# Moving transposed-tile and V copies from ScalarE to VectorE, and the feed-forward work inside an attention block

## The chip, the cores and the metric

The kernel runs on 8 NeuronCores of one Trainium2 chip. Every core runs the same program on its own 4 sequences of the batch of 32. The time is device microseconds (us) of the slowest core, for one execution.

## What is computed

For x of shape (32, 2048, 1024), with four 1024 x 1024 attention matrices and a feed-forward layer of 3072 hidden columns whose int32 weights are scaled by 1/127:

```python
xn = _layernorm(x, axis=-1)
# s: attention of xn
q = _l2norm(proj(Wq)); k = _l2norm(proj(Wk)); v = proj(Wv)   # 16 heads of 64
attn = jnp.einsum('bhqd,bhkd->bhqk', q, k)
mask = (rel < 0) | (rel >= WINDOW)      # rel = key - query, WINDOW = 128
attn = softmax(attn + alibi, masked)
s = (attn @ v) @ Wo
# g: silu of the feed-forward layer of xn
g = _silu((_silu(xn @ wg.T) * (xn @ wu.T)) @ wd.T)
x = x + s * g
```

A query attends to itself and the 127 keys behind it in the sequence's order, so a block of 128 queries needs two blocks of 128 keys: its own and the next.

## The kernel before

**Tiles.** A core's 4 sequences of 2048 tokens are cut into tiles of 512 tokens, 4 per sequence, 16 in all (`n_iters`). Before the first tile a prologue transposes all weights to bf16 with TensorE and stores them in HBM scratch (`prep_attn`, `prep_gu`, `prep_wd`), normalizes the first two tiles' x and computes K and V of tile 0.

**One tile** (`tile(g, wq_s)`) does the following, in this order: Q of tile g (`proj_eh`, L484, then `norm_apply`, L439 to L452, then `kq_transpose`, L465 and L472); the layer-norm sums of tile g+2 (`ln_stats`, L369 to L395, only where g+2 is still a tile, so 14 times in the loop); K of tile g+1 the same way as Q; V of tile g+1 (`proj_eh`, L484, and a copy out of PSUM, L724); four attention blocks of 128 queries (`attn_qb`); the layer norm's application for tile g+2 (`ln_apply`, L401 and L406) and its transposition (`xn_T`, L420 and L427); the 12 down-projection groups (`down_group`, L550); and the epilogue (`epilogue_tc`, L565 to L573), whose ScalarE and VectorE work runs beside the next tile's Q projection.

**The filler.** `filler(n)` puts n feed-forward units (`ffn_unit`) into the program at the place where it is called. A unit is 8 gate matmuls into PSUM tensor psB (L507), a Silu on ScalarE (L515) that reads them, 8 up matmuls (L524), and a multiplication on VectorE (L532) that writes HID. Each tile has 24 units. Two units alternate between two banks each of psB; all else of a tile uses psA.

**One attention block** (`attn_qb(g, qb, wo_s, filler)`). `ci` is 0 for the queries' own block of keys and 1 for the next one. The last block of a sequence has no second block of keys; that is 4 of the 64 blocks. For each ci, 16 score matmuls (L596) write all four banks of psA, four exponentials on ScalarE (L606) read one bank each and write PT, and four multiplications on VectorE (L611) put the position factors EB on PT. Then 32 matmuls with V (L627) write psA again, VectorE takes the reciprocal of the sums (L640) and normalizes into TM (L645), TensorE transposes TM (8 matmuls, L657), ScalarE copies that to AOF (L664), 16 matmuls with Wo follow (L673), and ScalarE copies their two banks to SBS (L681). Three filler calls stand in a block: behind the exponentials of each ci, and behind L645.

**What sets the order.** There is no scheduler. `_Plan.op` appends every operation to its engine's list in the order in which the Python code is run, and each engine works through its list strictly in that order. A wait is a `wait_ge` on a semaphore ahead of the instruction. It comes from the buffers that an operation reads and writes: `bpsA[b]` and `bpsB[b]` stand for the PSUM banks, `bPT`, `bTM4`, `bXN`, `bKF`, `bQF`, `bVP`, `bHID12` for the SBUF tensors. So the place of a filler call in the code sets its place in the lists of TensorE, ScalarE, VectorE and of the DMA queue at once. The tables of ScalarE's functions (L606, L515, L446 and L389 are listed with ACT_TABLE_LOAD) are put in by the compiler in front of an ACTIVATE whose function is not in the table set that is loaded.

Of the kernel before, what the change touches and what calls it, by code (L numbers as in the profile page):

```python
# [20 lines left out]
DCN = D // 128  # L21
# [107 lines left out]
def build_nc(n_iters=NTILES, dbg=False):  # L129
# [29 lines left out]
    P = _Plan()  # L159
# [6 lines left out]
    with stack:  # L166
# [246 lines left out]
        def xn_T(gt, tcs):  # L413
            p1 = gt % 2
            for tc in tcs:
                def tfn(e, tc=tc):
                    last = None
                    bc = psA[:, 512 * tc:512 * tc + 512].bitcast(BF16)
                    for dc in range(DCN):
                        last = e.transpose(  # L420
                            bc[:, 128 * dc:128 * dc + 128],
                            TM[:, 1024 * tc + 128 * dc:1024 * tc + 128 * dc + 128],
                            IDT[:, :])
                    return last
                P.op("pe", tfn, reads=[bTM4[tc], bIDT], writes=[bpsA[tc]],
                     tag=f"xnT{gt}_{tc}")
                P.op("act", (lambda e, tc=tc, p1=p1: e.copy(  # L427
                    XN[p1][:, :].rearrange("p (dc t) -> p dc t", dc=DCN)[:, :, 128 * tc:128 * tc + 128],
                    psA[:, 512 * tc:512 * tc + 512].bitcast(BF16).rearrange(
                        "p (dc t) -> p dc t", dc=DCN))),  # L430
                    reads=[bpsA[tc]], writes=[bXN[p1][tc]], tag=f"xnEv{gt}_{tc}")

        def norm_apply(g1, which, eh, tc):
# [25 lines left out]
        def kq_transpose(g1, DST, bDST, tag, tcs):  # L459
            for tc in tcs:  # L460
                def tfn(e, tc=tc):
                    last = None
                    bc = psA[:, 512 * tc:512 * tc + 512].bitcast(BF16)
                    for ec in range(DCN):
                        last = e.transpose(  # L465
                            bc[:, 128 * ec:128 * ec + 128],
                            TM[:, 1024 * tc + 128 * ec:1024 * tc + 128 * ec + 128],
                            IDT[:, :])
                    return last
                P.op("pe", tfn, reads=[bTM4[tc], bIDT], writes=[bpsA[tc]],  # L470
                     tag=f"{tag}{g1}_{tc}")
                P.op("act", (lambda e, tc=tc, DST=DST: e.copy(  # L472
                    DST[:, :].rearrange("p (ec t) -> p ec t", ec=DCN)[:, :, 128 * tc:128 * tc + 128],
                    psA[:, 512 * tc:512 * tc + 512].bitcast(BF16).rearrange(
                        "p (ec t) -> p ec t", ec=DCN))),
                    reads=[bpsA[tc]], writes=[bDST], tag=f"{tag}Ev{g1}_{tc}")

        def proj_eh(g1, eh, wslot, p1, tag):
# [104 lines left out]
        def attn_qb(g, qb, wo_s, filler):  # L583
            p, pn = g % 2, (g + 1) % 2
            j = g % TILES_PER_SEQ
            have_c1 = (qb < 3) or (j < 3 and g + 1 < n_iters)
            for ci in range(2 if have_c1 else 1):
                kc = qb + ci
                kpar, kcc = (p, kc) if kc < TCN else (pn, 0)
                for par in range(2):  # L590
                    def skfn(e, par=par, kpar=kpar, kcc=kcc, qb=qb):
                        last = None
                        r0 = 64 * par
                        for h in range(par, 16, 2):
                            ecb = 512 * (h // 2)
                            last = e.matmul(  # L596
                                psA[:, 128 * h:128 * h + 128],
                                KF[kpar][r0:r0 + 64, ecb + 128 * kcc:ecb + 128 * kcc + 128],
                                QF[r0:r0 + 64, ecb + 128 * qb:ecb + 128 * qb + 128],
                                start=True, stop=True)  # L600
                        return last
                    P.op("pe", skfn, reads=[bKF[kpar], bQF],
                         writes=[bpsA[0], bpsA[1], bpsA[2], bpsA[3]],
                         tag=f"qk{g}_{qb}_{ci}_{par}")
                for b in range(4):
                    P.op("act", (lambda e, b=b, ci=ci: e.activation(  # L606
                        PT[:, 2048 * ci + 512 * b:2048 * ci + 512 * b + 512],
                        psA[:, 512 * b:512 * b + 512], AF.Exp)),
                        reads=[bpsA[b]], writes=[bPT[ci][b]],
                        tag=f"exp{g}_{qb}_{ci}_{b}")  # L610
                    P.op("dve", (lambda e, b=b, ci=ci: e.tensor_tensor(  # L611
                        PT[:, 2048 * ci + 512 * b:2048 * ci + 512 * b + 512],
                        PT[:, 2048 * ci + 512 * b:2048 * ci + 512 * b + 512],
                        EB[:, 2048 * ci + 512 * b:2048 * ci + 512 * b + 512],
                        ALU.mult)),
                        reads=[bEB, bPT[ci][b]], writes=[bPT[ci][b]],
                        tag=f"emul{g}_{qb}_{ci}_{b}")
                filler(1)

            for b in range(4):  # L620
                def avfn(e, b=b, qb=qb, have_c1=have_c1, p=p, g=g):
                    last = None
# [25 lines left out]
                st(RZ0, 16).unsqueeze(2).broadcast_to([128, 16, 64]), ALU.mult)),  # L648
                reads=[bpsA[0], bpsA[1], bpsA[2], bpsA[3], bRZ],
                writes=[bTM4[qb]], tag=f"aonrm{g}_{qb}")  # L650
            filler(1)

            def aotfn(e, qb=qb):
                last = None
# [32 lines left out]
        def tile(g, wq_s):  # L687
            p, pn = g % 2, (g + 1) % 2
# [6 lines left out]
            def filler(n):  # L695
                for _ in range(n):
                    if fstate[0] < HCN:
                        ffn_unit(g, fstate[0], pf)
                        fstate[0] += 1
# [13 lines left out]
            if g + 1 < n_iters:  # L713
# [7 lines left out]
                wv_s = load_wa("wv", 0, f"wv0_{g}"), load_wa("wv", 1, f"wv1_{g}")  # L721
                for eh in range(2):
                    for tc in proj_eh(g + 1, eh, wv_s[eh], pn, "vproj"):
                        P.op("act", (lambda e, eh=eh, tc=tc, pn=pn: e.copy(  # L724
                            VP[pn][:, :].rearrange("p (kc h c) -> p kc h c", kc=4, c=65)[:, tc, 8 * eh:8 * eh + 8, 0:64],
                            psA[:, 512 * tc:512 * tc + 512].rearrange(
                                "p (h c) -> p h c", h=8))),
                            reads=[bpsA[tc]], writes=[bVP[pn]],
                            tag=f"vEv{g}_{eh}_{tc}")
                    filler(1)  # L730
# [36 lines left out]
            if has_ln:  # L767
                xn_T(g + 2, range(TCN))
# [50 lines left out]
        wv_s = load_wa("wv", 0, "wv0_p"), load_wa("wv", 1, "wv1_p")  # L819
        for eh in range(2):  # L820
            for tc in proj_eh(0, eh, wv_s[eh], 0, "vproj"):
                P.op("act", (lambda e, eh=eh, tc=tc: e.copy(
                    VP[0][:, :].rearrange("p (kc h c) -> p kc h c", kc=4, c=65)[:, tc, 8 * eh:8 * eh + 8, 0:64],
                    psA[:, 512 * tc:512 * tc + 512].rearrange(
                        "p (h c) -> p h c", h=8))),
                    reads=[bpsA[tc]], writes=[bVP[0]], tag=f"vEvp_{eh}_{tc}")
        prep_attn("wq")
        prep_attn("wo")
# [77 lines left out]
```

How the kernel before makes its waits and increments, by code:

```python
        def load_wa(nm, eh, tag):  # L226
            s = wa_i[0] % 3
            wa_i[0] += 1
            ap, bf = WA[s], bWA[s]
            src_ap = wT[nm][eh]
            P.op("sp", (lambda e, sem, ap=ap, src_ap=src_ap:
                        e.dma_start(ap[:, :], src_ap).then_inc(sem, 16)),
                 reads=[bWT[nm]], writes=[bf], tag=tag)
            return ap, bf
# [4 lines left out]
        def load_gu_hc(nm, hc, tag):  # L239
            s = gu9_i[0] % 9
            gu9_i[0] += 1
            ap, off = WGU[s // 3], 1024 * (s % 3)
            bf = bGU9[s]
            P.op("sp", (lambda e, sem, ap=ap, off=off, src=wT[nm][hc]:
                        e.dma_start(ap[:, off:off + 1024], src).then_inc(sem, 16)),
                 reads=[bWT[nm]], writes=[bf, bWGU[s // 3]], tag=tag)
            return (ap, off), bf
# [591 lines left out]
        def run(eng_obj, name):  # L839
            for (waits, fn, evt, tag, nd) in P.ops[name]:
                for w in waits:
                    eng_obj.wait_ge(sems[w.sem], w.val)
                if nd > 0:
                    fn(eng_obj, sems[evt.sem])
                else:
                    inst = fn(eng_obj)
                    if evt.used:
                        inst.then_inc(sems[evt.sem], 1)
            if name == "gp":
                for i in range(NDMASEM):
                    s_ = f"gp{i}"
                    if counts.get(s_, 0):
                        eng_obj.wait_ge(sems[s_], counts[s_])
```

## Time and profile before

| what | value |
|---|---|
| time before, median of 2 runs | 4488.03 us (4459.62 to 4516.44) |
| the profiled execution | 4467.43 us |
| its span on the slowest core | 4465.9 us (cores 4438.0 to 4465.9) |
| mean granted TensorE clock, cores 0 to 7 | 0.924 to 0.928 |
| busy: TensorE matmul, ScalarE, VectorE | 78%, 45%, 27% |

The profile is one execution seen by the hardware profiler. PE is TensorE's matmuls, PEld its weight loads, ACT is ScalarE, DVE is VectorE, POOL is GpSimd. L484 is line 484 of the kernel. A matmul's duration is its latency: matmuls overlap, so 8 matmuls of 128x512 that are listed with 380 ns each take 1.9 us together. The span begins with the prologue (about 600 us) and then has 16 tiles of about 249 us each.

### The profile page before, as it was taken

To read this page: it belongs to the slowest core of one execution; us is meant where nothing else is said; L and a number is where in the kernel's file an instruction comes from. 1 tells how busy PE (TensorE), PEld (TensorE's weight loads), DVE (VectorE), ACT (ScalarE), POOL (GpSimd) and SP (SyncE) were. 2 spreads that over 40 slices of the span, in tenths; PEclk is the share of its full clock that TensorE was granted. 3 is DMA by queue.
4 is the path that set the end of the run, shared out by engine and by line. 5 is a ranking of instruction groups with operands and counts; after the bars stand their busy time and mean duration, and the time that the engine had idled before them with its cause. 6 is when DMAs were issued, how large, how long until landed. Compare 5 with 4: busy or idle time off the path is not lost.

```text
span 4465.9 us, 59790 instructions; the slowest of 8 cores (4438.0 to 4465.9 us)
## 1 busy us (share of the span) xinstructions
PE 3499.2 (78%) x20160; PEld 1670.1 (37%) x20160; DVE 1219.4 (27%) x2230; ACT 1989.2 (45%) x2803; POOL 127.6 (3%) x276
## 2 busy tenths in 40 slices
PE   1422298888879888888888888888879888888887
PEld 1221144343434344343434343443434343444443
DVE  0100032323323232323333232323232232324141
ACT  4322163544635263544535363635545353635352
POOL 1111000000000000000000000000000000000000
PEclk9755599999999999999999999999999999999999
DMA  6576543434343433434343534434343534334342
GB/s 151 113 132 112 140 142 116 160 110 153 116 158 112 165 125 126 152 111 164 111 144 111 184 114 139 147 114 161 111 155 106 172 114 151 137 102 171 99 150 91
DMA packets 276419, 596.38 MB, mean 134 GB/s; under 512 B 71072, under 2 KB 71072, under 8 KB 258720
## 3 DMA queue, kind: packets, MB, share of 16 engines
q1 hardware_dynamic: 236192, 464.63, 32.4%
q0 software_dynamic: 39936, 127.94, 10.9%
q8 instruction: 175, 2.87, 0.3%
q14 instruction: 116, 0.95, 0.1%
HBM read 558.92 MB, written 60.82 MB: 139 GB/s over the span
## 4 chain that ended last, share of the span: by engine, by line
PE 56%; DMA 13%; ACT 12%; issue 9%; DVE 8%; POOL 0%; DVEq 0%; ACTq 0%; SPq 0%; POOLq 0%
PE psB L507 12%; PE psB L524 11%; PE psA L484 8%; PE psA L550 7%; PE psB L550 6%; PE psA L673 5%; DMA WD<-wdT_s 4%; PE psA L596 3%; DVE STAT L442 3%; DMA wgT_s<-WGU 2%; DMA wuT_s<-WGU 2%; PE psA L627 2%; DVE GBUF L569 2%; ACT GBUF L373 2%; ACT GBUF L369 2%
## 5 line engine op out<-in xcount | busy, mean ns | idle before, releaser
L484 PE MATMUL psA<-WA,XN 128*128 128x512 bf16 x3072 | 744.8, 403 | 243.9 <-DVE TM L452 177.5
L524 PE MATMUL psB<-XN,WGU 128*128 128x512 bf16 x3072 | 732.3, 382 | 31.9 <-ACT GBUF L565 29.7
L507 PE MATMUL psB<-XN,WGU 128*128 128x512 bf16 x3072 | 727.1, 380 | 3.8 <-ACT GBUF L565 3.8
L484 PEld LDWEIGHTS psA<-WA,XN 128*128 128x128 bf16 x3072 | 309.4, 102 | 673.3 <-issue 366.2
L550 PE MATMUL psA<-WD,HID 128*128 128x512 bf16 x1536 | 404.0, 386 | 96.3 <-ACT XN L427 38.7
L532 DVE TENSOR_TENSOR HID<-psB,TSC 128x512 bf16<-128x512 f32 x384 | 262.5, 691 | 726.5 <-PE psB L524 340.5
L524 PEld LDWEIGHTS psB<-XN,WGU 128*128 128x128 bf16 x3072 | 300.3, 98 | 401.7 <-issue 45.8
L507 PEld LDWEIGHTS psB<-XN,WGU 128*128 128x128 bf16 x3072 | 283.5, 98 | 331.2 <-issue 10.7
L550 PE MATMUL psB<-WD,HID 128*128 128x512 bf16 x1536 | 403.5, 386 | 0.0
L565 ACT ACTIVATE GBUF<-psA,CST 128x1024 f32<-128x1024 f32 x32 | 35.6, 1113 | 822.9 <-PE psB L550 777.2
L611 DVE TENSOR_TENSOR PT<-PT,EB 128x512 bf16<-128x512 bf16 x496 | 210.6, 425 | 565.4 <-ACT PT L606 541.9
L442 DVE TENSOR_REDUCE STAT<-SQ 128x8 f32<-128x512 f32 x256 | 173.3, 677 | 590.4 <-ACT SQ L439 590.1
L569 DVE TENSOR_TENSOR GBUF<-GBUF,SBS 128x1024 f32<-128x1024 f32 x64 | 78.4, 1226 | 902.6 <-ACT GBUF L565 902.6
L515 ACT ACTIVATE TSC<-psB,CST 128x512 bf16<-128x512 f32 x384 | 258.8, 686 | 141.8 <-PE psB L507 78.9
L673 PE MATMUL psA<-WA,AOF 128*128 128x512 bf16 x1024 | 231.3, 379 | 88.8 <-ACT AOF L664 88.8
L550 PEld LDWEIGHTS psA<-WD,HID 128*128 128x128 bf16 x1536 | 138.6, 98 | 324.3 <-issue 192.8
L606 ACT ACTIVATE PT<-psA 128x512 bf16<-128x512 f32 x496 | 256.0, 603 | 1.4
L278 PE MATMUL psA<-IDT,WD 128*128 128x128 bf16 x640 | 79.8, 304 | 225.0 <-DMA WD<-wg 50.6
L515 ACT ACT_TABLE_LOAD x186 | 238.6, 1283 | 3.6
L550 PEld LDWEIGHTS psB<-WD,HID 128*128 128x128 bf16 x1536 | 152.6, 99 | 189.0 <-issue 13.4
L606 ACT ACT_TABLE_LOAD x124 | 159.1, 1283 | 113.3 <-PE psA L596 112.2
L596 PE MATMUL psA<-QF,KF 64*128 64x128 bf16 x1984 | 149.9, 215 | 62.5 <-ACT SBS L681 42.4
(67 smaller groups left out, 2484.9 us busy)
## 6 DMA issues: line engine op xcount, KB each, us to landing
WGU<-wgT_s SPq DMA_DIRECT2D x384, 256.0 KB, 2.8
WGU<-wuT_s SPq DMA_DIRECT2D x384, 256.0 KB, 2.8
WD<-wdT_s SPq DMA_DIRECT2D x192, 512.0 KB, 3.6
XL<-x POOLq DMA_DIRECT2D x16, 2048.0 KB, 10.3
WA<-wkT_s SPq DMA_DIRECT2D x32, 1024.0 KB, 8.8
WA<-wvT_s SPq DMA_DIRECT2D x32, 1024.0 KB, 8.0
XE<-x POOLq DMA_DIRECT2D x16, 2048.0 KB, 9.8
WA<-wqT_s SPq DMA_DIRECT2D x32, 1024.0 KB, 6.0
```

What stands on the lines that cost most here:

```text
L442: P.op("dve", (lambda e, SS8=SS8, sqo=sqo: e.tensor_reduce(st(SS8, 8).rearrange("p (h u) -> p h u", u=1), SQ[:, sqo:sqo + 512].rearrange(" ...
L484: last = e.matmul(psA[:, 512 * tc:512 * tc + 512], XN[p1][:, 512 * dc + 128 * tc:512 * dc + 128 * tc + 128], wap[:, 512 * dc:512 * dc + 51 ...
L507: last = e.matmul(psB[:, go:go + 512], gap[:, goff + 128 * dc:goff + 128 * dc + 128], XN[p][:, 512 * dc:512 * dc + 512], start=(dc == 0), ...
L515: P.op("act", (lambda e, hc=hc, go=go: e.activation(TSC[:, 512 * (hc % 2):512 * (hc % 2) + 512], psB[:, go:go + 512], AF.Silu, scale=CST[: ...
L524: last = e.matmul(psB[:, uo:uo + 512], uap[:, uoff + 128 * dc:uoff + 128 * dc + 128], XN[p][:, 512 * dc:512 * dc + 512], start=(dc == 0), ...
L532: P.op("dve", (lambda e, hc=hc, uo=uo: e.tensor_tensor(HID[:, 512 * hc:512 * hc + 512], psB[:, uo:uo + 512], TSC[:, 512 * (hc % 2):512 * ( ...
L550: last = e.matmul(pt[:, off + 512 * dh:off + 512 * dh + 512], HID[:, 512 * hc + 128 * tc:512 * hc + 128 * tc + 128], wdap[:, 1024 * i + 51 ...
L569: P.op("dve", (lambda e, tc=tc: e.tensor_tensor(GBUF[:, :], GBUF[:, :], SBUF_S[:, 1024 * tc:1024 * tc + 1024], ALU.mult)), reads=[bG, bSB4 ...
L596: last = e.matmul(psA[:, 128 * h:128 * h + 128], KF[kpar][r0:r0 + 64, ecb + 128 * kcc:ecb + 128 * kcc + 128], QF[r0:r0 + 64, ecb + 128 * q ...
L606: P.op("act", (lambda e, b=b, ci=ci: e.activation(PT[:, 2048 * ci + 512 * b:2048 * ci + 512 * b + 512], psA[:, 512 * b:512 * b + 512], AF. ...
L611: P.op("dve", (lambda e, b=b, ci=ci: e.tensor_tensor(PT[:, 2048 * ci + 512 * b:2048 * ci + 512 * b + 512], PT[:, 2048 * ci + 512 * b:2048 ...
L673: last = e.matmul(psA[:, 1024 + 512 * half:1024 + 512 * half + 512], AOF[:, 128 * ec:128 * ec + 128], wap[:, 512 * ec:512 * ec + 512], sta ...
```

## The change

Two things are changed.

First, four copies out of PSUM go from ScalarE's list to VectorE's, at the same place in the program: the transposed layer norm output (L427), transposed Q and K (L472), V in the tile loop (L724) and V in the prologue (L822). `e.copy` on ScalarE becomes `e.tensor_scalar_mul` by 1.0 on VectorE.

Second, the three filler calls of an attention block move. The one behind the exponentials and EB multiplications of a ci now stands between the score matmuls and the exponentials of that ci, and the third, which stood behind the normalization L645, now stands ahead of the matmuls with V. Lines 606 to 645 of before are one higher in the changed kernel.

```diff
-                P.op("act", (lambda e, tc=tc, p1=p1: e.copy(
+                P.op("dve", (lambda e, tc=tc, p1=p1: e.tensor_scalar_mul(
                     XN[p1][:, :].rearrange("p (dc t) -> p dc t", dc=DCN)[:, :, 128 * tc:128 * tc + 128],
                     psA[:, 512 * tc:512 * tc + 512].bitcast(BF16).rearrange(
-                        "p (dc t) -> p dc t", dc=DCN))),
+                        "p (dc t) -> p dc t", dc=DCN), 1.0)),
                     reads=[bpsA[tc]], writes=[bXN[p1][tc]], tag=f"xnEv{gt}_{tc}")
...
@@ attn_qb
                         tag=f"qk{g}_{qb}_{ci}_{par}")
+                filler(1)
                 for b in range(4):
                     P.op("act", (lambda e, b=b, ci=ci: e.activation(
...
                         tag=f"emul{g}_{qb}_{ci}_{b}")
-                filler(1)
-
+
+            filler(1)
             for b in range(4):
                 def avfn(e, b=b, qb=qb, have_c1=have_c1, p=p, g=g):
...
                 writes=[bTM4[qb]], tag=f"aonrm{g}_{qb}")
-            filler(1)
 
             def aotfn(e, qb=qb):
```

L472, L724 and L822 are edited as L427 is.

**ScalarE's list, one attention block.** Before, from the exponentials of ci 0 to the copies into SBS (PT holds the exponentials, TSC is the Silu's output, AOF and SBS are the block's last copies):

```order
L606 ACTIVATE PT<-psA 128x512 x4
L515 ACTIVATE TSC<-psB,CST 128x512
L606 ACTIVATE PT<-psA 128x512 x4
L515 ACTIVATE TSC<-psB,CST 128x512 x2
L664 COPY AOF<-psA 128x1024
L681 CAST SBS<-psA 128x512 x2
```

The same block in the changed kernel:

```order
L515 ACTIVATE TSC<-psB,CST 128x512
L607 ACTIVATE PT<-psA 128x512 x4
L515 ACTIVATE TSC<-psB,CST 128x512
L607 ACTIVATE PT<-psA 128x512 x4
L515 ACTIVATE TSC<-psB,CST 128x512
L664 COPY AOF<-psA 128x1024
L681 CAST SBS<-psA 128x512 x2
```

Each Silu has moved from behind the four exponentials of its ci to ahead of them; the third is still behind the last exponentials.

**VectorE's list, one attention block.** Before, from the EB multiplications of ci 0 (PT<-PT,EB) to the third unit's multiplication into HID:

```order
L611 TENSOR_TENSOR PT<-PT,EB 128x512 x4
L532 TENSOR_TENSOR HID<-psB,TSC 128x512
L611 TENSOR_TENSOR PT<-PT,EB 128x512 x4
L532 TENSOR_TENSOR HID<-psB,TSC 128x512
L640 RECIPROCAL STAT<-psA 128x16
L645 TENSOR_TENSOR TM<-psA,STAT 128x1024
L532 TENSOR_TENSOR HID<-psB,TSC 128x512
```

The same block in the changed kernel:

```order
L532 TENSOR_TENSOR HID<-psB,TSC 128x512
L612 TENSOR_TENSOR PT<-PT,EB 128x512 x4
L532 TENSOR_TENSOR HID<-psB,TSC 128x512
L612 TENSOR_TENSOR PT<-PT,EB 128x512 x4
L532 TENSOR_TENSOR HID<-psB,TSC 128x512
L641 RECIPROCAL STAT<-psA 128x16
L646 TENSOR_TENSOR TM<-psA,STAT 128x1024
```

Each unit's multiplication stands ahead of the EB multiplications of its ci, and the third unit's has moved ahead of the reciprocal and the normalization.

**TensorE's list, from the matmuls with V to the next block's scores.** Before (L627 the matmuls with V, L657 the transposes, L673 the matmuls with Wo):

```order
L627 MATMUL psA<-VP,PT 128x65 x32
L507 MATMUL psB<-XN,WGU 128x512 x8
L524 MATMUL psB<-XN,WGU 128x512 x8
L657 MATMUL psA<-IDT,TM 128x128 x8
L673 MATMUL psA<-WA,AOF 128x512 x16
```

In the changed kernel, from the third unit on:

```order
L507 MATMUL psB<-XN,WGU 128x512 x8
L524 MATMUL psB<-XN,WGU 128x512 x8
L628 MATMUL psA<-VP,PT 128x65 x32
L657 MATMUL psA<-IDT,TM 128x128 x8
L673 MATMUL psA<-WA,AOF 128x512 x16
```

The unit that stood between the matmuls with V and the transposes of their normalized result now stands ahead of both. The score matmuls and the first two units keep their places in TensorE's list.

## Rows read from the trace of the kernel before

**Rows 1.** What TensorE waited for: us in total, times, longest us.

```profile
PE psA L484 <- DVE TM L452: 177.5, 33, 9.2
...
PE psA L550 <- ACT XN L427: 38.7, 14, 2.8
```

**Rows 2.** Timeline, one attention block: start, length, engine, instruction, [idle before <- releaser].

```profile
2420.77 0.60 PE L596 MATMUL psA<-QF,KF 64*128 64x128 bf16 x8 [0.88 <-ACT SBS L681]
...
2422.05 1.90 PE L507 MATMUL psB<-XN,WGU 128*128 128x512 bf16 x8
2422.20 1.28 ACT L606 ACT_TABLE_LOAD   x1 [1.58 <-PE psA L596]
2423.50 2.06 ACT L606 ACTIVATE PT<-psA 128x512 bf16<-128x512 f32 x4
...
2425.71 0.60 PE L596 MATMUL psA<-QF,KF 64*128 64x128 bf16 x8
...
2426.88 0.69 ACT L515 ACTIVATE TSC<-psB,CST 128x512 bf16<-128x512 f32 x1
...
2427.67 0.69 DVE L532 TENSOR_TENSOR HID<-psB,TSC 128x512 bf16<-128x512 f32 x1 [1.57 <-ACT TSC L515]
...
2428.88 2.06 ACT L606 ACTIVATE PT<-psA 128x512 bf16<-128x512 f32 x4
...
2429.57 1.90 DVE L611 TENSOR_TENSOR PT<-PT,EB 128x512 bf16<-128x512 bf16 x4 [1.22 <-ACT PT L606]
...
2430.46 1.66 PE L627 MATMUL psA<-VP,PT 128*128 128x65 bf16 x32
...
2431.96 1.89 PE L507 MATMUL psB<-XN,WGU 128*128 128x512 bf16 x8
...
2433.72 0.25 DVE L640 RECIPROCAL STAT<-psA 128x16 f32<-128x16 f32 x1
2434.06 0.69 ACT L515 ACTIVATE TSC<-psB,CST 128x512 bf16<-128x512 f32 x1 [1.12 <-DVE STAT L640]
2434.07 1.23 DVE L645 TENSOR_TENSOR TM<-psA,STAT 128x1024 bf16<-128x1024 f32 x1
...
2435.55 0.61 PE L657 MATMUL psA<-IDT,TM 128*128 128x128 bf16 x8
...
2437.51 3.61 PE L673 MATMUL psA<-WA,AOF 128*128 128x512 bf16 x16 [1.35 <-ACT AOF L664]
...
2442.00 1.36 PE L596 MATMUL psA<-QF,KF 64*128 64x128 bf16 x16 [0.88 <-ACT SBS L681]
```

**Rows 3.** Timeline of the same tile and the next: waits around the normalizations.

```profile
2472.45 1.02 PE L550 MATMUL psA<-WD,HID 128*128 128x512 bf16 x4 [2.76 <-ACT XN L427]
...
2538.72 6.59 PE L484 MATMUL psA<-WA,XN 128*128 128x512 bf16 x22 [4.33 <-DVE TM L452]
...
2558.63 4.31 ACT L472 COPY QF<-psA 128x1024 bf16<-128x1024 bf16 x4
...
2563.41 1.06 ACT L369 ACTIVATE GBUF<-XL 128x1024 f32<-128x1024 f32 x1
...
2581.13 10.01 PE L484 MATMUL psA<-WA,XN 128*128 128x512 bf16 x32 [8.82 <-DVE TM L452]
```

**Rows 4.** Groups by line and shape: busy us, mean ns of one, idle before.

```profile
L611 DVE TENSOR_TENSOR PT<-PT,EB 128x512 bf16<-128x512 bf16 x496 | 210.6, 425 | 565.4 <-ACT PT L606 541.9
...
L645 DVE TENSOR_TENSOR TM<-psA,STAT 128x1024 bf16<-128x1024 f32 x64 | 78.4, 1225 | 6.7
...
L472 ACT COPY QF<-psA 128x1024 bf16<-128x1024 bf16 x64 | 64.8, 1012 | 4.3
```

**Rows 5.** Stretches: length, busy us (instructions) of each engine, clock, DMA share, GB/s.

```profile
2535.00:2540.00 5.00, 1.27 (x5) 0.61 (x6) 2.35 (x7) 2.71 (x5) 1.21 (x2) 0.93 0.63 227
2540.00:2545.00 5.00, 5.00 (x19) 1.88 (x17) 3.62 (x10) 1.56 (x5) 0.08 (x1) 0.73 0.55 170
...
2470.00:2475.00 5.00, 2.55 (x12) 1.20 (x13) 0.00 (x0) 2.20 (x3) 0.00 (x0) 1.00 0.86 349
```

More of the change, by code:

```diff
@@ L471, in kq_transpose @@
                      tag=f"{tag}{g1}_{tc}")
-                P.op("act", (lambda e, tc=tc, DST=DST: e.copy(
+                P.op("dve", (lambda e, tc=tc, DST=DST: e.tensor_scalar_mul(
                     DST[:, :].rearrange("p (ec t) -> p ec t", ec=DCN)[:, :, 128 * tc:128 * tc + 128],
                     psA[:, 512 * tc:512 * tc + 512].bitcast(BF16).rearrange(
-                        "p (ec t) -> p ec t", ec=DCN))),
+                        "p (ec t) -> p ec t", ec=DCN), 1.0)),
                     reads=[bpsA[tc]], writes=[bDST], tag=f"{tag}Ev{g1}_{tc}")
@@ L723, in tile @@
                     for tc in proj_eh(g + 1, eh, wv_s[eh], pn, "vproj"):
-                        P.op("act", (lambda e, eh=eh, tc=tc, pn=pn: e.copy(
+                        P.op("dve", (lambda e, eh=eh, tc=tc, pn=pn: e.tensor_scalar_mul(
                             VP[pn][:, :].rearrange("p (kc h c) -> p kc h c", kc=4, c=65)[:, tc, 8 * eh:8 * eh + 8, 0:64],
                             psA[:, 512 * tc:512 * tc + 512].rearrange(
-                                "p (h c) -> p h c", h=8))),
+                                "p (h c) -> p h c", h=8), 1.0)),
                             reads=[bpsA[tc]], writes=[bVP[pn]],
@@ L821, in build_nc @@
             for tc in proj_eh(0, eh, wv_s[eh], 0, "vproj"):
-                P.op("act", (lambda e, eh=eh, tc=tc: e.copy(
+                P.op("dve", (lambda e, eh=eh, tc=tc: e.tensor_scalar_mul(
                     VP[0][:, :].rearrange("p (kc h c) -> p kc h c", kc=4, c=65)[:, tc, 8 * eh:8 * eh + 8, 0:64],
                     psA[:, 512 * tc:512 * tc + 512].rearrange(
-                        "p (h c) -> p h c", h=8))),
+                        "p (h c) -> p h c", h=8), 1.0)),
                     reads=[bpsA[tc]], writes=[bVP[0]], tag=f"vEvp_{eh}_{tc}")
```

## The prediction

> **What bounds the kernel now.** I read the table of waits for TensorE first, then the timeline of one attention block, then the places where the moved copies stand. TensorE is busy for 78% of the span and ScalarE for 45%, so the tile loop is TensorE work with holes in it, and the question is which holes the change closes and which it opens. The reader should see two things in the waits [rows 1]. The largest one, 177.5 us, is the projections (L484) waiting for the normalization L452, a chain of ScalarE and VectorE steps. The down projections wait 38.7 us, 14 times, for ScalarE's copy of XN (L427), one of the copies that are moved.
>
> The timeline of one block [rows 2] shows an order that fits well. Take the first score matmul at 2420.77 as zero; the next block's is at 2442.00, so a block takes 21.23. The gate starts at 1.28, ScalarE does its table load and the four exponentials meanwhile, and the second scores start at 4.94 (2425.71), 0.15 after the last exponential has ended (2423.50 + 2.06 = 2425.56). The unit of 3.46 us (2427.00 to 2430.46) covers the exponentials, and the third unit covers reciprocal and normalization: the transposes follow at 2435.55, 3.59 after that unit's gate. TensorE's only holes in the block are 1.35 ahead of L673 and 0.88 ahead of the next scores.
>
> **The attention block after the change.** TensorE keeps scores, unit, scores, unit in the same order, but the second scores need all four banks of psA, so they need the first four exponentials, and on ScalarE these now stand behind a Silu that needs the gate. I follow the chain with the durations of rows 2. Gate at 1.28; its Silu starts 2.10 after a gate does (2431.96 to 2434.06), so 3.38. The Silu table is loaded already, since the unit before was the last to need one. Silu 0.69, table load 1.30 (2422.20 to 2423.50), exponentials 2.06, release 0.15: the second scores start at 7.58 in place of 4.94. That is a first step of 2.64 lost.
>
> From there: gate 1.29 later at 8.87; ScalarE can go on 2.10 later, at 10.97, and now needs a table load ahead of the Silu (12.27), the Silu (12.96), a load (14.26), the exponentials (16.32), a load again, and the third Silu at 17.62, whose gate has long ended. Its multiplication into HID starts 0.79 after the Silu does (2426.88 to 2427.67), 18.41. VectorE works in order, and behind this multiplication now stand the reciprocal (19.10), the normalization 0.35 later (19.45) and so the transposes 1.48 later (2434.07 to 2435.55), at 20.93. The matmuls with V have been done by then: their last operand is ready at 14.26 + 0.69 + 1.90 = 16.85, and they end near 17.4. From transposes to the next block's scores nothing changes, 6.45 (2435.55 to 2442.00). The block ends at 27.38 in place of 21.23: 6.15 more.
>
> The number of table loads stays four per block. What changes is that all four lie on the path, and that the third unit covers the exponentials while nothing covers the normalization. 60 blocks have two halves: 60 x 6.15 = 369. The 4 blocks at a sequence's end have one, and I take the first step for them, 4 x 2.6 = 10. The lower bound for a block is 5.2, if the waits turn out some 0.2 shorter at each of five hand-overs; the upper one is 6.5.
>
> **The copies.** No row shows VectorE reading bf16 from PSUM. Bounds: 1.23 us as L645 (1024 elements from fp32 PSUM), and twice the 512 elements of L611 at 0.425, so 0.85 or, as part of 0.425 is fixed, somewhat less; ScalarE takes 1.012 [rows 4]. L611 is the nearest row by type, and I take 0.7 to 0.85.
>
> At XN (14 times, where ln_stats runs) the copies end the wait of 2.76 [rows 3]. At 0.75 each the four end about 0.8 earlier, at 1.23 about 1.2 later: -11 us, bounds -11 and +17. The last unit's multiplication is ahead of them on VectorE; that is counted.
>
> At Q, ScalarE spends 4.31 on four copies, then takes a unit's Silu, then starts ln_stats at 2563.41. Once the copies are gone, the Silu can run as soon as its gate ends: that gate follows the transposes at about 2558.3, so 2560.4 by the 2.10 above, and ln_stats starts at about 2561.1, 2.3 earlier. The chain behind it ends in the wait of 8.82 at 2581.13 [rows 3], so this wait becomes 6.5: 14 x 2.3 = -32 us. Bounds: 0, if TensorE then waits for something else in that place, and -60, if the whole 4.31 counts. VectorE has no other work there until the squares come.
>
> K's copies and V's are hidden before and after: each is followed by a unit of 3.46 us or stands beside 7 us of projections, and a bank's copy needs 0.85 to 1.23. I cost them at 0, and the prologue's too. If the cover went, a tile would lose at most the 0.2 by which each copy could be slower.
>
> **TensorE's clock.** The hole between the end of the matmuls with V and the transposes will be 3.5 us, followed by only 0.6 of work and 1.35 of waiting. Rows show a wait of 2.76 without any fall (the stretch 2470 to 2475, clock 1.00), and a wait of 4.33 that ends at 2538.72 with the granted clock falling to its lower level (1.2 GHz) around there: 0.93 and 0.73 in two stretches of 5 us, which is 0.7 + 2.7 = 3.4 us at half [rows 3, 5]. Mine lies between. If the fall comes in each of the 60 blocks, with TensorE at work throughout, the 3.4 us cost 1.7 each, 102 us; if it never comes, 0. Part of such a stretch falls into the wait ahead of L673, so I take 1.0 each, +60. By the Trainium skill, "TensorE: Matmul & The Clock Gate", section "HAM oscillation — how this bites in real kernels", it is gaps that bring the engine down again and again and each burst then starts cold, which speaks for this term; the trace agrees at the 4.33 us wait.
>
> **Sum.** Against the profiled execution, 4467.4: + 369 + 10 - 11 - 32 + 60 = 4863, I say 4860. That execution lies 0.5% under the median of the two runs shown (4488), inside their spread.
>
> **The rivals.**
> A. Only the first step counts: VectorE's late third multiplication is hidden, because the third unit on TensorE runs late enough to cover it. 60 x 2.64 + 10 = 168, - 43: 4592. Against it: the unit ends at 15.8, and the reciprocal waits till 19.1.
>
> B. Not slower: ScalarE is what limits each tile, and every wait that its copies end or push goes. Place: the waits of rows 1, 177.5 + 38.7 = 216. With A's 158 for the blocks: 4467 + 158 - 216 = 4409. It decides where a block loses less than 216 / 60 = 3.6. For it: ScalarE's copies stand ahead of both waits. Against it: the wait of 8.82 holds ln_stats itself, of which no part is moved, and that of 4.33 comes behind no moved copy.
>
> C. The clock stays at the lower level through the attention blocks. Then the two gates that are on the chain take 1.7 more each, the scores 0.6 twice and L673 3.2: 8 per block, 4863 - 60 + 480 = 5280. Against it: the other holes are 2.64 and shorter, like the 2.76 without a fall.
>
> D. A table load costs more than its row. The Trainium skill, "ScalarE: Activation LUTs", section "What ACT_TABLE_LOAD costs", has a drain of about 1.38 us behind each load of 1.28. In this kernel that would put 4 x 1.38 on each block's chain, x 60 = 331: 5190 as an estimate from that page. The trace disagrees: the exponentials start 1.30 after the load does [rows 2]. As a mechanism of rows alone, a second cost as long as the load itself, 4 x 1.28 x 60 = 307, gives 5170.
>
> That the change doesn't do what it says can be excluded: the order of the lists shows it.
>
> **Chances.** Forecast 0.83, A 0.06, B 0.04, C 0.04, D 0.03. For the forecast's own range, low: blocks at 5.2 (-57), no fall of the clock (-60), 4746; high: blocks at 6.5 (+21), the clock in full (+42), copies at 1.23 (+28), 4954. Range 4745 to 4950, which leaves out A to D. Faster by over 2% (about what a measurement of this kernel can tell from no change) 0.01, a part of B; within 2% 0.03, the rest of B; slower 0.96.
>
> **What would show it.** In the profile after: the second scores wait 2.6 for the exponentials (L607), about 160 us in all, a wait that the kernel of before does not have. The transposes L657 wait about 3.5 for L646, some 200 us in all. The third Silu starts 17.6 after the block's first score, a block takes 27.4, and the projections' wait for L452 falls from 177.5 to about 145. The copies on VectorE show 0.7 to 0.85 us. The clock's mean falls below 0.92 if the clock term is right. I am wrong if a block takes under 25 us, if the Silu's table load runs ahead of its wait for the gate (that would take 1.3 off each block), or if the clock in the attention stretches stays at 1.00 (then 4800).

## The result, and the profile after

The changed kernel takes 5039 us (median of 12 executions; 5034.6 to 5042.7 in the undisturbed eight of them) against 4545 for the kernel before in the same comparison (lowest 4451.6). The ratio is 1.1306, 95% interval [1.1291, 1.1322]: 13% slower. The prediction had the sign and the place right, with 4860 us, but its size too small: the time lies above the range's end of 4950. (In some executions of every kernel here, before and after alike, part of the cores show a lower granted clock for long stretches; ratios leave those executions out, and "undisturbed cores" are those of an execution that do not show it.)

The page of the changed kernel, its head, its clock by slices and the busy times:

```profile
span 5038.6 us, 59650 instructions; the slowest of 8 cores (5015.2 to 5038.6 us)
...
PE 3764.0 (75%) x20160; PEld 1759.6 (35%) x20160; DVE 1429.6 (28%) x2550; ACT 1733.5 (34%) x2483; POOL 127.6 (3%) x276
...
PEclk9655889898998989898998989899898989899988
```

ScalarE is 256 us less busy than before, VectorE 210 more, as moved. TensorE has the same 20160 matmuls and is busy 265 us longer. That is the clue: the same matmuls take longer, and the mean granted clock of TensorE is 0.873 on this core, where before has 0.927. The traces of these two profiles show only two levels of the clock, full (2.4 GHz) and half (1.2 GHz), so the time at half can be worked out: (1 - 0.873) x 2 x 5038.6 = 1280 us, before (1 - 0.927) x 2 x 4465.9 = 652.

What TensorE waited for in the changed kernel (us in total, times, longest), which answers to [rows 1]:

```profile
PE psA L657 <- DVE TM L646: 210.9, 64, 3.7
PE psA L596 <- ACT PT L607: 159.6, 60, 2.9
PE psA L484 <- DVE TM L452: 151.9, 34, 6.8
...
PE psA L550 <- DVE XN L427: 26.3, 14, 2.2
```

The first two did not exist before, but for 0.3 us. They are 210.9 / 64 = 3.3 and 159.6 / 60 = 2.7 each, where 3.5 and 2.64 were predicted. The two others have shrunk by 25.6 and 12.4.

One attention block of the changed kernel, from one block's first scores to the next's, which answers to [rows 2]:

```profile
2621.21 1.37 PE L596 MATMUL psA<-QF,KF 64*128 64x128 bf16 x16
...
2622.51 1.90 PE L507 MATMUL psB<-XN,WGU 128*128 128x512 bf16 x8
...
2624.62 0.69 ACT L515 ACTIVATE TSC<-psB,CST 128x512 bf16<-128x512 f32 x1 [4.17 <-PE psB L507]
2625.33 1.28 ACT L607 ACT_TABLE_LOAD   x1
...
2628.83 2.17 PE L596 MATMUL psA<-QF,KF 64*128 64x128 bf16 x16 [2.69 <-ACT PT L607]
...
2630.93 3.59 PE L507 MATMUL psB<-XN,WGU 128*128 128x512 bf16 x8
...
2634.72 1.28 ACT L515 ACT_TABLE_LOAD   x1 [6.03 <-PE psB L507]
...
2641.39 0.69 ACT L515 ACTIVATE TSC<-psB,CST 128x512 bf16<-128x512 f32 x1
2642.18 0.69 DVE L532 TENSOR_TENSOR HID<-psB,TSC 128x512 bf16<-128x512 f32 x1 [1.57 <-ACT TSC L515]
2642.79 0.25 DVE L641 RECIPROCAL STAT<-psA 128x16 f32<-128x16 f32 x1
...
2644.62 0.61 PE L657 MATMUL psA<-IDT,TM 128*128 128x128 bf16 x8 [3.35 <-DVE TM L646]
...
2646.69 6.44 PE L673 MATMUL psA<-WA,AOF 128*128 128x512 bf16 x16 [1.46 <-DMA WGU<-wgT_s]
...
2654.01 1.36 PE L596 MATMUL psA<-QF,KF 64*128 64x128 bf16 x16 [0.88 <-ACT SBS L681]
```

Read against the steps: the second scores start at 7.62 (2628.83 - 2621.21), predicted 7.58. Until then the chain is exact. Then the same 16 score matmuls take 2.17 in place of 1.37, and the 8 gate matmuls 3.59 in place of 1.90. From here each thing is late by what the slow matmuls add: the second Silu's table load comes at 13.5 (predicted 10.97), the transposes at 23.4 (20.93). And behind the second wait the 16 matmuls with Wo take 6.44 in place of 3.61. (The 1.46 ahead of them is the usual wait for AOF, 0.1 longer for a transfer that came last.) The block is 32.8 long; the prediction said 27.4 by the steps and added 1.0 for the clock. It is one of the longer blocks: over the 48 blocks of this trace that have two halves and another block right behind them, the mean from first scores to first scores is 31.6.

The stretches of this block (length, busy us of PE, PEld, DVE, ACT and POOL, clock, DMA share, GB/s) show the granted clock:

```profile
2621.21:2631.00 9.79, 6.80 (x50) 4.00 (x50) 3.08 (x6) 4.04 (x6) 0.00 (x0) 0.87 0.44 146
2631.00:2645.00 14.00, 10.65 (x72) 5.10 (x72) 4.48 (x8) 7.29 (x9) 0.00 (x0) 0.84 0.37 114
2645.00:2654.00 9.00, 6.67 (x21) 2.23 (x18) 0.00 (x0) 2.19 (x3) 0.00 (x0) 0.62 0.10 29
```

Half-speed time is twice the missing share: 2.5, 4.5 and 6.8 us, together 13.8 of 32.8.

The copies on VectorE (busy us, mean ns, idle before):

```profile
L724 DVE TENSOR_SCALAR VP<-psA 128x512 bf16<-128x512 f32 x120 | 83.3, 694 | 119.8 <-PE psA L484 119.8
...
L472 DVE TENSOR_SCALAR QF<-psA 128x1024 bf16<-128x1024 bf16 x64 | 44.1, 689 | 5.4 <-DVE QF L472 0.5
```

0.689 us for 1024 bf16 elements from PSUM, just under the low end of what was taken (0.7 to 0.85), where ScalarE took 1.012. V's copies from fp32 take 0.694 on VectorE, ScalarE needed 0.587, and nothing waits for them.

### The profile page after: what moved, and what is told of

It reads as the page before. It is cut to its first block, busy times and chain, and to the rows that moved or that the text cites. A ratio compares the mean times of both kernels' runs of the same rounds, so it can differ in the third digit from the quotient of the medians.

```text
span 5038.6 us, 59650 instructions; the slowest of 8 cores (5015.2 to 5038.6 us)
## 1 busy us (share of the span) xinstructions
PE 3764.0 (75%) x20160; PEld 1759.6 (35%) x20160; DVE 1429.6 (28%) x2550; ACT 1733.5 (34%) x2483; POOL 127.6 (3%) x276
## 4 chain that ended last, share of the span: by engine, by line
PE 43%; ACT 22%; DMA 12%; DVE 11%; issue 10%; DVEq 0%; ACTq 0%; POOL 0%; SPq 0%; POOLq 0%
PE psB L507 10%; PE psA L673 7%; PE psA L484 6%; PE psA L550 5%; PE psB L550 5%; ACT PT L607 4%; DMA WD<-wdT_s 4%; ACT L515 4%; PE psA L596 3%; PE psB L524 3%; ACT L607 3%; DVE STAT L442 3%; ACT TSC L515 3%; DMA wgT_s<-WGU 2%; DMA wuT_s<-WGU 2%
## 5 line engine op out<-in xcount | busy, mean ns | idle before, releaser
L507 PE MATMUL psB<-XN,WGU 128*128 128x512 bf16 x3072 | 821.8, 416 | 4.1 <-ACT GBUF L565 4.1
L524 PE MATMUL psB<-XN,WGU 128*128 128x512 bf16 x3072 | 756.1, 391 | 29.7 <-ACT GBUF L565 29.7
L524 PEld LDWEIGHTS psB<-XN,WGU 128*128 128x128 bf16 x3072 | 310.0, 101 | 432.0 <-issue 101.4
L507 PEld LDWEIGHTS psB<-XN,WGU 128*128 128x128 bf16 x3072 | 306.8, 104 | 407.2 <-issue 118.6
L673 PE MATMUL psA<-WA,AOF 128*128 128x512 bf16 x1024 | 361.3, 530 | 88.7 <-ACT AOF L664 85.8
L596 PE MATMUL psA<-QF,KF 64*128 64x128 bf16 x1984 | 178.2, 240 | 220.2 <-ACT PT L607 159.6
L596 PEld LDWEIGHTS psA<-QF,KF 64*128 64x128 bf16 x1984 | 134.0, 104 | 298.2 <-issue 298.2
L673 PEld LDWEIGHTS psA<-WA,AOF 128*128 128x128 bf16 x1024 | 126.2, 128 | 305.8 <-issue 274.3
```

The lines of the kernel that those rows point to most:

```text
L507: last = e.matmul(psB[:, go:go + 512], gap[:, goff + 128 * dc:goff + 128 * dc + 128], XN[p][:, 512 * dc:512 * dc + 512], start=(dc == 0), ...
L524: last = e.matmul(psB[:, uo:uo + 512], uap[:, uoff + 128 * dc:uoff + 128 * dc + 128], XN[p][:, 512 * dc:512 * dc + 512], start=(dc == 0), ...
L596: last = e.matmul(psA[:, 128 * h:128 * h + 128], KF[kpar][r0:r0 + 64, ecb + 128 * kcc:ecb + 128 * kcc + 128], QF[r0:r0 + 64, ecb + 128 * q ...
L673: last = e.matmul(psA[:, 1024 + 512 * half:1024 + 512 * half + 512], AOF[:, 128 * ec:128 * ec + 128], wap[:, 512 * ec:512 * ec + 512], sta ...
```

## The experiments

The theory after the result: the chain is as predicted, and what was too small is the clock. Each of a block's two waits brings it down, and the matmuls that follow are on the chain. The rival: the chain through ScalarE and VectorE itself is longer, and the low clock only goes with idling. A second question was what each part of the change costs alone.

**The two parts alone.** `copies_only` undoes the filler calls:

```diff
-                filler(1)
                 for b in range(4):
                     P.op("act", (lambda e, b=b, ci=ci: e.activation(
...
                         tag=f"emul{g}_{qb}_{ci}_{b}")
-
-            filler(1)
+                filler(1)
             for b in range(4):
...
                 writes=[bTM4[qb]], tag=f"aonrm{g}_{qb}")
+            filler(1)
```

> The four copies on VectorE, the filler calls where they were. Theory (the moved filler calls are the whole loss, and the copies a small gain): the projections' wait for L452 goes from 177.5 to about 150 and the wait for XN from 38.7 to about 26, so 4415 us, ratio about 0.99. Rival (VectorE's copies are part of the loss, by delaying the HID multiplications): above 4480.

Measured: ratio 0.9881, interval [0.978, 0.9982], lowest execution 4402 us against 4453 for the kernel before in the same comparison. On core 2 of its profile (4411 us) the waits are 151.1 for L452 and 25.8 for XN, as expected. The theory holds, and the copies are a gain of about 50 us, though by the interval it could be almost nothing or 2%.

`fillers_only` is the kernel of before with the three filler calls moved as in the change.

> The copies stay on ScalarE, the three filler calls moved. Theory: the copies' gain of about 40 us is missing, 5080 us. Rival (copies and fillers act on each other, ScalarE being the longer for its copies only now): 5150 or more.

Measured: 5207 us, with two cores at 5204 and 5206 and the six others at 5078 to 5110. The four cores without any disturbed stretch are at 5078 to 5093, and on these the theory's 5080 is met. It is one profile of two executions, so it is weaker than the others. But the two parts add up within some 10 us: 5035 + 50 = 5085.

**Which filler call.** `third_back` takes the changed kernel and puts only the third call back behind the normalization:

```diff
-            filler(1)
             for b in range(4):
                 def avfn(e, b=b, qb=qb, have_c1=have_c1, p=p, g=g):
...
                 writes=[bTM4[qb]], tag=f"aonrm{g}_{qb}")
+            filler(1)
```

> The changed kernel with the third filler call back behind L646; the two others stay ahead of the exponentials. Theory (the late exponentials make the loss, and the third unit only decides where the hole stands): the matmuls with V start at about 16.9 after the block's first scores where the changed kernel has its transposes at 23.4, the hole of 3 us moves ahead of them, the block stays above 30 us, 4950 to 5040 us. Rival (the third call's place costs the 3.3 us of the wait ahead of L657 by itself): 211 us less, 4830.

Measured: 4951 and 4970 us, ratio 1.1091 [1.0991, 1.119]. What TensorE waited for in it:

```profile
PE psA L627 <- DVE PT L612: 172.1, 66, 3.4
PE psA L596 <- ACT PT L607: 157.7, 60, 2.7
```

The wait of 210.9 ahead of the transposes is gone, and 172.1 stand ahead of the matmuls with V instead: the hole moved by one step. So with the exponentials late, the third call's place decides where the second hole is, and not whether there is one.

`pair_back` is the reverse: the ci calls back, the third call ahead of the matmuls with V.

```diff
-                filler(1)
                 for b in range(4):
                     P.op("act", (lambda e, b=b, ci=ci: e.activation(
...
                         tag=f"emul{g}_{qb}_{ci}_{b}")
+                filler(1)
```

> The changed kernel with the two calls of the ci loop back behind the EB multiplications; the third call stays ahead of the matmuls with V. By the rows of before the third unit's up ends at 13.1, the matmuls with V at 14.7, reciprocal and normalization at 16.4 and the transposes start at 16.7 in place of 14.8: a block of 23.1. Theory: 4415 + 64 x 1.9 = 4535 us, and no fall of the clock in the blocks (hole of 2.0). Rival (the third call costs its 3.3 us whatever the others do, and a fall of the clock with it): 4700.

Measured: 4668 us, undisturbed cores 6 and 7 at 4585 and 4586; two executions only, so no ratio. Two waits of its profile:

```profile
PE psA L484 <- DVE TM L452: 149.5, 34, 7.0
PE psA L657 <- DVE TM L646: 125.9, 64, 2.3
```

125.9 / 64 = 2.0 per block, as worked out (1.9). But core 6 has a clock of 0.908, so (1 - 0.908) x 2 x 4584.8 = 844 us at half, some 200 more than before. My claim that a hole of 2.0 makes no fall was wrong, and the time is 50 us above the 4535 on the best cores. The rival's 4700 is missed too, but its fall of the clock is there. On core 6 the clock is at half in 60 of the 64 blocks, somewhere between the matmuls with V and the end of those with Wo. One of them, with the wait of 1.94 ahead of L657 and, 0.6 of matmuls later, one of 1.68 ahead of L673:

```profile
2428.96 0.61 PE L657 MATMUL psA<-IDT,TM 128*128 128x128 bf16 x8 [1.94 <-DVE TM L646]
2431.24 5.08 PE L673 MATMUL psA<-WA,AOF 128*128 128x512 bf16 x15 [1.68 <-ACT AOF L664]
```

The same block on core 0 has the same two waits and keeps its clock (15 matmuls of L673 in 3.40 us, granted clock 1.00):

```profile
2430.78 0.61 PE L657 MATMUL psA<-IDT,TM 128*128 128x128 bf16 x8 [1.95 <-DVE TM L646]
...
2433.07 3.40 PE L673 MATMUL psA<-WA,AOF 128*128 128x512 bf16 x15 [1.68 <-ACT AOF L664]
```

The parts of the move overlap. Against the 4402 of `copies_only`, the third call alone costs about 180 us (4585), the other two alone about 550 (`third_back`, 4951), and all three together 633.

**The clock by itself.** Four kernels leave the changed kernel's order as it is and give TensorE idle matmuls in the waits, whose result nobody reads. They write the psB bank that the next gate writes, which is free by then. The code is shortened here:

```diff
+        def idle_mm(n):
+            bank = fs_ref[0][0] % 2
+            def dmf(e, n=n, bank=bank):
+                for _ in range(n):
+                    last = e.matmul(psB[:, 512 * bank:512 * bank + 512],
+                                    IDT[:, :], EB[:, 0:512], start=True, stop=True)
+                return last
+            P.op("pe", dmf, reads=[bIDT, bEB], writes=[bpsB[bank]], tag="idle")
...
                 filler(1)
+                if ci == 0 and have_c1:
+                    idle_mm(11)
                 for b in range(4):
...
                 writes=[bTM4[qb]], tag=f"aonrm{g}_{qb}")
+            idle_mm(15)
```

> The changed kernel with idle matmuls (128x512, into the psB bank that the next gate writes, their result is not used) on TensorE in the two waits of a block with two halves: 11 (2.4 us) ahead of the second scores and 15 (3.2 us) between the matmuls with V and the transposes, the latter in all 64. They make nothing wait that does not wait already. Theory (the two waits bring TensorE's clock to its lower level, and the work of the chain that then runs at half speed is the part of the loss that the prediction had too small): clock back to 1.00 in the blocks, a block of 27.4 to 27.6, 4790 to 4810 us. Rival (the chain through ScalarE and VectorE is longer than predicted, and the lower clock only goes with idling): 5030 us or more, since work was added.

Measured: 4792 to 4806 us, ratio 1.0713 [1.0609, 1.0818]. Some 1600 matmuls were added and 240 us have gone. The theory's number is met within its range, and the rival is out: over the 48 blocks of core 0 that have two halves and another block right behind them, a block takes 27.35 us on average, and the steps of the prediction gave 27.38. Core 0's clock, and the second wait of a block in its timeline, where L589 is the idle matmuls:

```profile
core 0: 4789.3 us, clock 0.939
```

```profile
2601.12 3.40 PE L589 MATMUL psB<-EB,IDT 128*128 128x512 bf16 x15
...
2604.38 0.61 PE L674 MATMUL psA<-IDT,TM 128*128 128x128 bf16 x8
...
2606.34 3.61 PE L690 MATMUL psA<-WA,AOF 128*128 128x512 bf16 x16 [1.35 <-ACT AOF L681]
```

The matmuls with Wo take 3.61 again. At half: (1 - 0.939) x 2 x 4789.3 = 584 us on core 0, up to 614 on the three other undisturbed cores, where the cores of the changed kernel have 1244 to 1289. So 630 to 705 us at half speed cost 243 us of time, 0.34 to 0.39 of each. All of it on the chain would cost 0.5 of each, since work that fills a us at half speed takes half a us at full; so some 70 to 80% of it was on the chain, and the rest fell on waits or beside it.

`hole1` fills only the wait ahead of the second scores.

> Only the 11 idle matmuls ahead of the second scores. Theory: the fall behind this wait goes (scores, gate and up of the second half at full speed, at most 2.3 us of a block), that behind the transposes' wait stays: about 4920 us. Rival (the clock follows the mean load of the block): no change in one half, the same small rise in both, 5000 us or more.

Measured: 4951 us (lowest; the profiled execution 4994, its six undisturbed cores at 4925 to 4933), ratio 1.111 [1.0976, 1.1245]. `hole2` fills only the wait ahead of the transposes.

> Only the 15 idle matmuls ahead of the transposes. Theory: L673 back from 6.4 us to 3.6, up to 3 us of a block, the fall behind the exponentials' wait stays: about 4900 us. Rival as for the kernel with the first wait filled: 5000 us or more.

Measured: 4863 and 4873, ratio 1.0877 [1.077, 1.0984]. Against the 5035 of the changed kernel the first gives back 84 us (about 100 on undisturbed cores) and the second 172, where both filled give 243. So the two falls are nearly independent, and both were wanted to get the whole. I had expected 115 and 135: the second costs more than the first, because it hits L673, which stands wholly on the chain. Its 16 matmuls take 5.8 us on average in `hole1` and 3.6 in `hole2` (core 0 of each).

The traces show which blocks have time at half speed. Out of 64 blocks (60 of which have the first wait), on the core with the fewest and the one with the most:

| kernel | from the first scores to the matmuls with V | from there to the end of Wo |
|---|---|---|
| before | 0 to 1 | 0 |
| changed | 56 to 59 | 64 |
| `hole1` | 0 | 64 |
| `hole2` | 31 to 50 | 0 to 1 |
| both filled (`both_holes`) | 0 to 1 | 0 to 2 |
| half of each (`half_holes`, next) | 9 to 13 | 10 to 16 |

Each fall goes with its own wait, and the rival of the mean load is out. Filling the second wait also saves some blocks the first fall.

`half_holes` fills half of each wait (6 and 8 idle matmuls).

> The changed kernel with idle matmuls for half of each wait of a block: 6 (1.3 us) ahead of the second scores and 8 (1.7 us) ahead of the transposes, so 1.3 and 1.6 us of waiting stay. Theory (it is the uninterrupted wait of 2.7 and 3.3 us that brings the clock down): no falls in the blocks, as with both waits filled, 4800 us. Rival (any idle time in the block adds to the falls, in proportion): about half of the 240 us, 4910 us.

Measured: 4829 to 4840 us, ratio 1.0843 [1.0819, 1.0866]. So 206 of the 243 us come back with half of each wait filled; the theory's 4800 and the rival's 4910 are both missed, the theory by 30. Some falls are left. One block of it:

```profile
2613.14 0.61 PE L674 MATMUL psA<-IDT,TM 128*128 128x128 bf16 x8 [1.34 <-DVE TM L662]
...
2615.11 5.30 PE L690 MATMUL psA<-WA,AOF 128*128 128x512 bf16 x16 [1.35 <-ACT AOF L681]
```

Two waits of 1.34 and 1.35, with 0.61 of transposes between them, and L673's matmuls (L690 here) at 5.30 in place of 3.61. But most blocks of this trace have waits of the same size (1.6 and 1.35 in the middle) and no fall: on core 0 it is 28 of 64 blocks that have time at half speed. So neither expectation holds. Shorter waits make falls rarer, and whether a given block has one can't be told from its own waits.

**VectorE's order.** `mult_behind` moves only the third unit's multiplication into HID behind the normalization; TensorE and ScalarE are as in the change.

```diff
+            late = []
-            filler(1)
+            filler(1, late)
             for b in range(4):
                 def avfn(e, b=b, qb=qb, have_c1=have_c1, p=p, g=g):
...
                 writes=[bTM4[qb]], tag=f"aonrm{g}_{qb}")
+            for mult in late:
+                mult()
```

> The changed kernel with the third unit's HID multiplication alone moved behind the normalization L646 on VectorE; TensorE's and ScalarE's lists as in the changed kernel. Theory (VectorE's strict order holds reciprocal and normalization behind a multiplication that waits for the late Silu): the reciprocal follows the last matmul with V at about 17.5, the transposes come 1.7 earlier, the wait ahead of them falls from 3.3 to about 1.7 in all 64 blocks, and some of the half-speed time goes too: 4890 to 4930 us. Rival (ScalarE's queue, not VectorE's, sets the end of the block, through the third Silu ahead of the copy to AOF): no change, 5030 us.

Measured: 4930 us, ratio 1.1023 [1.0937, 1.111]. Its waits, on core 2:

```profile
PE psA L601 <- ACT PT L612: 159.2, 60, 2.9
...
PE psA L665 <- DVE TM L652: 124.7, 64, 2.1
```

The wait ahead of the transposes (L665 here) falls from 210.9 to 124.7, the first one stays: 86 us of waits, 105 of time. The theory holds and the rival is out. A multiplication that nobody was in need of held up the normalization through its place in the list.

**A version that beats both.** With the copies gone, ScalarE waits up to 9.67 us at a time while V is computed (the timeline of the changed kernel), and in K it is still the 10 us of ln_stats that the projections wait for. `ln_later` has the copies on VectorE, the fillers as before, and moves ln_stats behind K:

```diff
-            if has_ln:
-                ln_stats(g + 2)
-
             if g + 1 < n_iters:
...
                 kq_transpose(g + 1, KF[pn], bKF[pn], "kT", range(TCN))
                 filler(1)
+                if has_ln:
+                    ln_stats(g + 2)
```

> The four copies on VectorE, the filler calls as before, and ln_stats moved from ahead of K to between K and V, where ScalarE has waits of 9.7 us with the copies gone. Theory (ScalarE's work in that place is what the projections wait for in K): that wait of 6.5 goes in 14 tiles, -90 us, and the half-speed stretch behind it too, about -50: 4270 us. Rival (the chain then ends in V, since the Silus of the units wait behind ln_stats): 4380 us or more.

Measured: 4252 us (lowest), ratio 0.9523, interval [0.9468, 0.9577]: 4.8% faster than before, and the cores at clocks of 0.939 to 0.944. The waits and a core's clock:

```profile
PE psA L673 <- ACT AOF L664: 88.7, 64, 1.7
PE psA L484 <- DVE TM L452: 58.3, 18, 4.3
```

```profile
core 0: 4250.5 us, clock 0.943
```

The theory had 4270, and the rival is out. The projections' wait is 58.3 in place of 177.5 [rows 1]; what is left is that of Q. Of the 150 us gained over `copies_only` 94 are this wait (152.4 there). The traces have 478 to 524 us at half speed in place of 576 to 622, some 100 less, which can be worth 50 at most. That fits the rest, but no run separates it here.

`ln_later_act` makes the same move with the copies on ScalarE.

> The kernel of before with only ln_stats moved in the same way; the copies stay on ScalarE. Theory (the move pays only with the copies on VectorE): V's copies wait behind some 13 us of ln_stats, the second half of V's projections waits for them about 6 us, and the gain of the K wait is given back: 4400 us or more. Rival (the copies do not matter): as ln_later plus the 45 us of the copies, 4315 us.

Measured: 4373 us, ratio 0.9817 [0.9726, 0.9908], between the two expectations and nearer to the theory. So the move alone gains about 80 us (4455 before, lowest in the same comparison): the gain was not given back whole, as the theory had it. Its waits, on core 2, show the price:

```profile
PE psA L484 <- ACT VP L723: 69.2, 14, 5.1
PE psA L484 <- DVE TM L452: 59.7, 23, 4.5
```

V's second half waits 5 us for V's copies in each of 14 tiles, a wait that `ln_later` does not have. So the copies are worth about 50 us alone and about 120 once ln_stats has moved.

`ln_later_idle` adds 18 idle matmuls in Q's wait.

> ln_later with 18 idle matmuls (3.9 us) in Q, in the wait of 4.33 us ahead of the second half of the projections. Theory (the clock falls behind every wait of that length): the half-speed time in Q goes, up to 3.4 us at half in 16 tiles, so 15 to 30 us less than ln_later. Rival: same or slower, if the idle matmuls hold the projections up.

Measured: ratio 0.9523 [0.9477, 0.9569], 4254 to 4267 us: no difference to `ln_later`, though the cores' clocks are 0.946 to 0.953 in place of 0.939 to 0.944. The theory's 15 to 30 us did not come; the rival's "same" is what was measured. If half-speed time behind that wait costs anything, it is less than this comparison shows, whose interval is about 20 us either way.

## Why the prediction was wrong

**The chain held.** The two waits are 2.69 and 3.35 against 2.64 and 3.5, and the second scores come at 7.62 against 7.58. Behind them every start is late by the slow matmuls, so the rest of the chain can only be read with the clock kept up: in `both_holes` a block takes 27.35 against 27.38, and the time is 4792 to 4806 against 4803, which is the prediction's sum without its clock term.

**The copies held.** XN: 12.4 us less waiting for the 11 predicted. Q and K: K's wait is 6.45 where 6.5 was predicted, and the waits for L452 are 25.6 less in total for 32. At XN the shorter wait also keeps the clock: it is 2.8 to 3.1 before and 1.8 to 2.2 after, and the clock fell in it or within 2 us behind it in 82 of 112 cases before (14 tiles on 8 cores) and in 6 of 111 in the changed kernel. The prediction did not have that. The timeline of the changed kernel has the start of ln_stats and K's wait:

```profile
2559.84 1.05 ACT L369 ACTIVATE GBUF<-XL 128x1024 f32<-128x1024 f32 x1
...
2577.58 7.63 PE L484 MATMUL psA<-WA,XN 128*128 128x512 bf16 x27 [6.45 <-DVE TM L452]
```

From the one to the other are 17.74 us, and 17.72 in [rows 3] (2563.41 to 2581.13): the chain between them is unchanged and has only been started earlier. `copies_only` is at 4402 to 4411 for 4467 - 43 = 4424.

**The step that failed is the size of the clock term:** 1.0 us for each of 60 blocks, 60 us, upper bound 102. The runs show 243, 4.0 per block. Three things in it were wrong.

First, the count. I let only the wait ahead of the transposes make a fall and wrote that 2.64 "and shorter" is like the 2.76 [rows 3] behind which the clock stayed at 1.00. `hole1` and `hole2` show one fall for each wait. And the reading was of one tile out of 14: [rows 3] and [rows 5] show the exception. On core 0 of the same trace the same wait of 2.76 brought the clock down in 12 of 14 tiles, and over all cores waits of 2.76 to 3.14 in that place did so in 82 of 112. One of them:

```profile
974.52 1.95 PE L420 MATMUL psA<-IDT,TM 128*128 128x128 bf16 x32
979.23 1.70 PE L550 MATMUL psA<-WD,HID 128*128 128x512 bf16 x4 [2.76 <-ACT XN L427]
980.72 1.91 PE L550 MATMUL psB<-WD,HID 128*128 128x512 bf16 x4
```

```profile
976.00:979.00 3.00, 0.47 (x9) 0.29 (x6) 0.00 (x0) 2.98 (x4) 0.00 (x0) 1.00 1.03 294
979.00:983.00 4.00, 3.77 (x10) 1.44 (x11) 0.00 (x0) 0.00 (x0) 0.00 (x0) 0.57 0.81 241
```

Four matmuls take 1.70 and then 1.91 in place of 1.02 and 1.03, at a granted clock of 0.57. The trace that the prediction was made from already said that waits of this length usually bring the clock down.

Second, the length. I took 3.4 us of half speed from the one place in [rows 5]. The changed kernel has 630 to 705 us more of it than with both waits filled, about 11 per block.

Third, the share on the chain. I argued that part falls into the wait ahead of L673. But with Wo's matmuls at half speed that wait is over and all 16 are on the chain: 6.44 for 3.61 in the block shown, 5.64 on average on that core, so 2.0 us in this one step.

The upper bound broke for the same reasons: it allowed one stretch of 3.4 us per block, so it bounded the loss inside a stretch but not the number of stretches.

**The rivals.** A is out: both waits stand in the trace. B is out: the waits that it meant to end shrank by 25.6 and 12.4 of their 216. Its mechanism shows in `ln_later` instead, where ScalarE's work was really taken out of K's way. C, the clock low through the whole block, goes too far (5280), but the truth is between it and the forecast: 13.8 of 32.8 us in the block shown. It had 0.04. D, a longer table load, is out: the row after a load starts 1.29 later in the changed kernel too (2625.33 to the exponentials at 2626.62). The chain's agreement in `both_holes` leaves no room for it. What I cited for the clock from the Trainium skill, "TensorE: Matmul & The Clock Gate", section "HAM oscillation — how this bites in real kernels", that each burst behind a gap starts cold again, pointed the right way: 64 of 64 blocks have half-speed time behind the second wait. I gave the trace's single example the greater weight in size.

## What to carry to other kernels

An independent piece of work put between a producer and its consumer helps only on the engine that has to wait; on every other engine in whose list it lands it can be a barrier, and here one filler call put a Silu that waits for 8 matmuls ahead of the exponentials, and a multiplication ahead of a normalization. When new waits of 2 to 3 us appear on TensorE several times per loop, count each as a fall of the clock, and price the matmuls behind it at up to double where they are on the chain. Before a row is used to say that a wait does no harm, look at every place of the trace that has the same wait: here one tile said no and twelve said yes. Moving work off an engine pays fully only when the next piece of that engine's work is moved into the room that it leaves: the copies alone gave 1.2%, ln_stats moved alone 1.8%, both together 4.8%.

## What was not expected of the hardware

Adding 11 and 15 matmuls per block that compute nothing made the changed kernel 240 us faster. Nearly the same (206 us) came with half of them.

The clock did not follow the length of a single wait. In one trace (before, core 0) a wait of 2.76 ahead of the down projections left it at 1.00 in 2 tiles [rows 3, 5] and was followed by half speed in 12, one of them shown above. What stands right in front is the same in the two tiles shown, nearly 2 us of unbroken transposes. In the tile of [rows 3] they are

```profile
2467.73 1.95 PE L420 MATMUL psA<-IDT,TM 128*128 128x128 bf16 x32
```

In the changed kernel waits of 2.7 and 3.3 us brought a fall in nearly every block, in `pair_back` waits of 1.95 and 1.7 in 60 of 64 (core 6), in `half_holes` waits of 1.3 to 1.7 in 28 of 64 (core 0). So longer waits make a fall more likely, and nothing in these rows says beforehand which block will have one. By the Trainium skill, "TensorE: Matmul & The Clock Gate", section "Part 1: The HAM clock gate", the clock is set by how busy the engine has been recently. The rows agree in so far as the last wait alone does not decide. What does was not measured here.
